# A Mamba block and a routed mixture of experts on one core: two of eight drive products moved to TensorE, and the start and end of the scan stage reordered

## The reference, cut to what matters

```python
h = layernorm(layernorm(x)) * g + b
x_in, z = split(h @ W_in)                      # 512 channels each
u = silu(causal_depthwise_conv(x_in, taps=4) + conv_b)
dt, B, C = split(u @ W_xproj)                  # 64, 16 and 16 columns
delta = softplus(dt @ W_dt + b_dt)
s[n] = exp(delta * A[n]) * s[n] + delta * u * B[n]     # 16 states n, over time
y = sum_n s[n] * C[n] + u * D
x1 = x + layernorm(x) + (y * silu(z)) @ W_out
# experts: each row of layernorm(x1) goes to its best 2 of 8 experts,
# relu(row @ W1 + b1) @ W2 + b2, weighed by a softmax of the two logits
out = x1 + layernorm(mixed + row) * gamma + beta
```

## Time and profile before

| | us |
|---|---|
| median of three runs (2540.58 to 2542.79) | 2542.03 |
| the profiled execution, its own time | 2553.05 |
| its span, first to last instruction | 2551.3 |
| first scan starts | 74.19 |
| last gate of the scan stage starts | 1890.67 |
| first tile of the experts is read | 1954.25 |
| busy: PE, DVE, ACT, POOL | 2055.1, 2123.9, 1408.2, 1965.7 |
| mean granted TensorE clock | 0.90 |

### The profile page before, as it was taken

How to read it: one execution, slowest core, us unless ns; L and a number is a source line. 1 busy time by engine, 2 the same in 40 slices (tenths; PEclk the granted TensorE clock), 3 DMA queues, 4 the chain that set the end, 5 groups by cost and what they waited for, 6 DMA issues and landing times. The chain is left out here.

```text
span 2551.3 us, 41205 instructions
## 1 busy us (share of the span) xinstructions
PE 2055.1 (81%) x11191; PEld 1561.7 (61%) x11192; DVE 2123.9 (83%) x3249; ACT 1408.2 (55%) x2909; POOL 1965.7 (77%) x1233
## 2 busy tenths in 40 slices
PE   6769687796968787796968787796754999999988
PEld 2446465564646555565646555564653999999973
DVE  1899999999999999999999999999962556555657
ACT  4666766767676766766675776766431222222216
POOL 1899899999999999999999999999962222222227
PEclk9889898898989798898989898898765999999999
DMA  3240413224040413214041413314034777777769
GB/s 102 87 150 10 141 57 126 85 91 157 18 167 33 151 51 124 102 74 166 21 155 35 149 60 116 113 55 166 11 120 139 223 227 230 227 227 231 227 197 332
DMA packets 177827, 328.42 MB, mean 129 GB/s; under 512 B 19539, under 2 KB 100979, under 8 KB 177556
## 3 DMA queue, kind: packets, MB, share of 16 engines
q1 hardware_dynamic: 147172, 274.00, 33.6%
q0 software_dynamic: 12624, 34.62, 3.6%
q10 hardware_dynamic: 17888, 18.11, 2.1%
HBM read 272.25 MB, written 54.41 MB: 128 GB/s over the span
## 5 line engine op out<-in xcount | busy, mean ns | idle before, releaser
L729 POOL TENSOR_TENSOR dbu<-du,bb 128x1024 f32<-128x1024 f32 x512 | 1199.0, 2355 | 13.4 <-DVE ps_a L564 9.0
L960 ACT ACTIVATE ps_a<-dl,a_neg 128x512 f32<-128x512 f32 x1024 | 683.0, 683 | 151.4 <-DVE wd L577 75.5
L1162 PEld LDWEIGHTS ps_y<-ident,wd 128*128 128x128 f32 x2816 | 376.5, 158 | 112.9 <-issue 82.9
L1162 PE MATMUL ps_y<-ident,wd 128*128 128x128 f32 x2816 | 425.6, 299 | 16.5 <-DVE wd L577 16.5
L564 DVE TENSOR_TENSOR_SCAN ps_a<-ps_a,carry,dbu 128x512 f32<-128x512 f32 x352 | 437.5, 1276 | 0.1
L1440 POOL DMA_INDIRECT eo_scratch<-ow,idx x135 | 129.9, 962 | 391.3 <-DVE ow L1394 385.4
L577 DVE TENSOR_TENSOR wd<-ps_a,rows_c 128x1024 f32<-128x1024 f32 (+1 forms) x384 | 426.9, 1112 | 0.0
L564 DVE TENSOR_TENSOR_SCAN ps_a<-ps_a,dbu 128x512 f32<-128x512 f32 x352 | 417.1, 1216 | 4.1 <-ACT ps_a L960 3.7
L746 POOL TENSOR_TENSOR wp<-ss,rows_c 128x1024 f32<-128x1024 f32 (+1 forms) x192 | 382.0, 1990 | 15.2 <-DVE ss L564 7.5
L1549 PE MATMUL e_ps_h<-xT,w 128*128 128x128 f32 x2160 | 264.9, 276 | 0.0
L1380 DVE TENSOR_SCALAR e_hT<-e_ps_h,b_turned 128x128 f32<-128x128 f32 x540 | 152.1, 344 | 134.7 <-PE e_ps_h L1549 133.7
(11 more groups left out here) (166 smaller groups left out, 2798.5 us busy)
## 6 DMA issues: line engine op xcount, KB each, us to landing
w<-in_L_ffn_W_dram SPq DMA_DIRECT2D x135, 512.0 KB
bb<-b_scratch SPq DMA_DIRECT2D x128, 512.0 KB, 4.3
rows_c<-b_scratch SPq DMA_DIRECT2D x128, 512.0 KB, 6.6
xt<-xs_scratch SPq DMA_DIRECT2D x135, 129.0 KB
ee<-eo_scratch SPq DMA_DIRECT2D x64, 256.0 KB, 7.2
xb<-in_L_attn_x_dram SPq DMA_DIRECT2D x16, 512.0 KB, 3.7
hx<-in_L_attn_x_dram SPq DMA_DIRECT2D x16, 512.0 KB, 5.4
x_scratch<-hx SPq DMA_DIRECT2D x16, 512.0 KB, 3.3
```

The lines of the kernel that those rows point to most:

```text
L729: pool.tensor_tensor(dbu[:, k % NBU], du[:, g % 2, :].unsqueeze(1).broadcast_to([P, 2, CH]), bb[:, 2 * m:2 * m + 2, :], ALU.mult).then_inc ...
L960: act.activation(ps_a[:, bank(k), :], dl[:, g, :], ACT.Exp, scale=a_neg[:, g, n:n + 1]).then_inc(exp_done, 1)
L1162: ins = pe.matmul(ps_y[:, i, :], wd[:, s % NWD, h, i * P:(i + 1) * P], ident[:], start=False, stop=False, is_transpose=True, skip_group_ch ...
```

## The change

- **Drive of four states from turned rows.** For the states 4, 5, 10 and 11 (the pairs 2 and 5, `BMS`) GpSimd makes no product. TensorE turns delta * u once a tile ("turnu", four transposes), ScalarE copies it to `duT`. Once a chunk TensorE turns the B rows ("bturn"), and ScalarE scales the identity by them, giving 16 diagonals (`diagonals`). `drive` multiplies the turned rows by the diagonals, 16 matrix products a tile, into the PSUM bank that took the decay before; the decay of these states goes to the ring `dbu` in SBUF. The scan takes them with their places exchanged.
- **State 15 is held.** VectorE has five pairs a tile to weigh, GpSimd three pairs, where it had two pairs and a single. Which bank a pair has now changes from tile to tile.
- **Residual and its statistics.** The residual row is added by TensorE with the identity inside "out"; ScalarE takes it out with its sum, and its squares with a second pass (`stats_x1` moves from VectorE to ScalarE).
- **Order.** `STEADY` and all offsets are new. The routing follows one chunk behind, not two. In the first tiles of chunk 0 the list `START` holds what no longer stands ahead of the first scan (z, the next h and x).
- **Start.** The first convolution is done on VectorE (`first_conv`); weights are loaded in three groups with semaphores of their own, some from ScalarE's queue, and W_in in two halves; ahead of the first scan stand two softplus and half the diagonals.
- **End.** `out_part` sums three of the four groups of the last output projection ahead of its last gate; the last "back" has a PSUM bank of its own; the second choice's rows of the last chunk have a buffer (`stage_b`); the padding transfers are issued half by SyncE, half by ScalarE.

The diff, cut to its core:

```diff
+    BMS = (2, 5)
+    NTP = len(BMS)
     HB = N // 2
+    NB = HB - NTP
...
-    DIRECT = (1, 4, 7, 10, 13, 15)
+    DIRECT = (1, 4, 7, 10, 13)
+    ND = len(DIRECT)
...
+        bb = sb("bb", [P, 2 * NB, CH])
+        dg = sb("dg", [P, NTP, 2, NT, P])
+        duT = sb("duT", [P, NT, P])
+        bT = sb("bT", [P, NT, NTP, 2])
...
+        stage_b = zt[:, NC % 2].rearrange("p i d -> p (i d)")[:, 0:NT * XW].rearrange("p (i d) -> p i d", i=NT)
...
-        FIRST = [("h", 0), ("h", 1), ("x", 0), ("x", 1), ("x", 2), ("x", 3), ("conv", 0), ("conv", 1), ("conv", 2),
-                 ("conv", 3), ("dbc", 0), ("dt", 0), ("dt", 1), ("z", 0), ("dt", 2), ("z", 1), ("dt", 3), ("z", 2),
-                 ("z", 3)]
...
+        FIRST = [("h", 0), ("h", 1), ("x", 0), ("x", 1), ("x", 2), ("x", 3), ("dbc", 0), ("bturn", 0), ("dt", 0),
+                 ("dt", 1), ("turnu", 0)]
+        START = [("z", 0, 0, 0, 1, 1), ("z", 1, 0, 0, 1, 2), ("z", 2, 0, 1, 1, 3), ("z", 3, 0, 2, 1, 4),
+                 ("h", 0, 1, 4, 1, 2), ("h", 1, 1, 5, 1, 2), ("x", 0, 1, 8, 1, 2), ("x", 1, 1, 10, 1, 2),
+                 ("turnu", 1, 0, 13, 1, 2)]
+        START_DIAGONALS = (2, 3)
+        END = [("back", 2, 0, 54, 1, 2)]
+        XL_LAST = NC * SG - 14
+        OUT_EARLY = NC * SG - 5
+        STEADY = [("h", 0, 1, 0, 1, 3), ("h", 1, 1, 1, 1, 5), ("x", 0, 1, 4, 2, 3), ("back", 3, -1, 6, 1, 2),
+                  ("dt", 2, 0, 9, 1, 2), ("out", 0, -1, 10, 1, 4), ("turnu", 1, 0, 10, 1, 5),
+                  ("out", 1, -1, 14, 2, 4), ("x", 1, 1, 17, 1, 5), ("conv", 0, 1, 18, 2, 2), ("conv", 1, 1, 21, 2, 5),
+                  ("x", 2, 1, 24, 2, 3), ("x", 3, 1, 25, 1, 4), ("dt", 3, 0, 29, 1, 2), ("conv", 2, 1, 27, 3, 5),
+                  ("turnu", 2, 0, 33, 1, 4), ("conv", 3, 1, 30, 4, 8), ("turnx", 0, -1, 37, 1, 4),
+                  ("turnx", 1, -1, 37, 1, 4), ("logit", 0, -1, 40, 1, 0), ("dbc", 0, 1, 41, 1, 4),
+                  ("back", 0, 0, 42, 1, 3), ("bturn", 0, 1, 43, 1, 3), ("rank", 0, -1, 43, 1, 1),
+                  ("back", 1, 0, 45, 1, 3), ("turnu", 3, 0, 47, 1, 1), ("dt", 0, 1, 48, 1, 1), ("dt", 1, 1, 49, 1, 2),
+                  ("z", 0, 1, 53, 2, 2), ("z", 1, 1, 54, 2, 4), ("z", 2, 1, 56, 2, 5), ("turnu", 0, 1, 59, 1, 2),
+                  ("z", 3, 1, 59, 2, 4), ("back", 2, 0, 60, 1, 4)]
+        HALO_AT = 0
...
+        DIAGONALS = (53, 59, 64, 64)
+        DRIVE = (4, 5, 10, 10)
+        KEEP_EARLY = (2, 9)
...
+            def first_conv(g):
+
+                dve.wait_ge(*emptied("x", g, 0))
+                dst = xslot(0, g)
+                dve.tensor_scalar(dst, xin[:, g, 0:CH], cw[:, g, 0:1], cb[:, g:g + 1], ALU.mult, ALU.add
+                                  ).then_inc(conv_step, 1)
+                for k in range(1, TAPS):
+                    dve.wait_ge(conv_step, TAPS * g + k)
+                    dve.scalar_tensor_tensor(dst, xin[:, g, k:k + CH], cw[:, g, k:k + 1], dst, ALU.mult, ALU.add
+                                             ).then_inc(conv_step, 1)
...
+                if n // 2 in BMS:
+                    dve.wait_ge(tb_done, driven(t, n))
+                elif n % 2 == 0:
+                    dve.wait_ge(dbu_done, products(t, n // 2))
...
-                dve.tensor_tensor_scan(dst, ps_a[:, bank(k), :], dbu[:, k // 2 % NBU, n % 2, :], init,
-                                       ALU.mult, ALU.add).then_inc(scan_done, 1)
+                pair = ps_a[:, bank(k), :], dbu[:, k // 2 % NBU, n % 2, :]
+                decay, drive = reversed(pair) if n // 2 in BMS else pair
+                dve.tensor_tensor_scan(dst, decay, drive, init, ALU.mult, ALU.add).then_inc(scan_done, 1)
...
-                if t <= LAST:
+                if t <= LAST and m not in BMS:
                     times_b(t, m)
...
+            def stats_x1(q, step):
+
+                if step == 0:
+                    for j in range(2):
+                        act.wait_ge(*emptied("out", j, q))
+                    if q > 0:
+                        act.wait_ge(prm1, q)
+                    act.mul(nm[:, 1, :], sums[:], -1.0 / D).then_inc(lnr_step, 1)
+                else:
+                    act.wait_ge(lnr_step, 2 * q + 1)
+                    if q > 0:
+                        if q < NC - 1:
+                            act.wait_ge(scat, 16 * 2 * NT * q)
+                        act.wait_ge(proj_full, full("turnx", 1, q - 1))
+                        act.wait_ge(proj_full, full("out", 1, q - 1))
+                    junk = rows_from(q, 1)
+                    for i in range(NT):
+                        ins = act.activation(junk[:, i, 0:D], hx[:, i, :], ACT.Square, bias=nm[:, 1, i:i + 1],
+                                             accum_out=sqs[:, i:i + 1])
+                    ins.then_inc(lnr_step, 1)
+
...
+                elif kind == "turnu":
+                    act.wait_ge(tb_done, 2 * NTP * (q * G + g))
+                    act.copy(duT[:].rearrange("p i d -> p (i d)"), src).then_inc(taken, 1)
+                elif kind == "bturn":
+                    act.wait_ge(dg_done, NTP * q)
+                    rows = src[:, 0:NT * 2 * N].rearrange("p (i n) -> p i n", i=NT)
+                    for p, b in enumerate(BMS):
+                        ins = act.copy(bT[:, :, p, :], rows[:, :, 2 * b:2 * b + 2])
+                    ins.then_inc(taken, 1)
+                elif kind == "out":
+                    for i in range(2 * g, 2 * g + 2):
+                        ins = act.activation(hx[:, i, :], src[:, (i - 2 * g) * D:(i - 2 * g + 1) * D], ACT.Copy,
+                                             accum_out=sums[:, i:i + 1])
+                    ins.then_inc(taken, 1)
                 else:
                     act.copy(zt[:, q % 2, :, g * P:(g + 1) * P], src.rearrange("p (i d) -> p i d", i=NT)
                              ).then_inc(taken, 1)
+
+            def diagonals(q, j):
...
+            def diagonals(q, j):
+
+                p = j // 2
+                act.wait_ge(*emptied("bturn", 0, q))
+                if q > 0:
+                    act.wait_ge(tb_done, 2 * (NTP * (G * q - 1) + p) + 2)
+                for i in range(2 * (j % 2), 2 * (j % 2) + 2):
+                    for h in range(2):
+                        ins = act.activation(dg[:, p, h, i, :], ident[:], ACT.Copy, scale=bT[:, i, p, h:h + 1])
+                if j % 2 == 1:
+                    ins.then_inc(dg_done, 1)
...
+                if n // 2 in BMS:
+                    dst = dbu[:, k // 2 % NBU, n % 2, :]
+                    if k // 2 >= NBU:
+                        act.wait_ge(scan_done, k - n % 2 - 2 * NBU + 2)
...
+                    if q == NC - 1:
+                        if part == parts - 1:
+                            ins = out_part(q, g, range(G - 1, G))
+                    for ik in range(2 * G * part // parts, 2 * G * (part + 1) // parts) if q < NC - 1 else ():
                         i, k = divmod(ik, G)
                         ins = pe.matmul(dst[:, i * D:(i + 1) * D], zt[:, q % 2, 2 * g + i, k * P:(k + 1) * P],
-                                        wout[:, k, :], start=(k == 0), stop=(k == G - 1))
+                                        wout[:, k, :], start=(k == 0), stop=False)
+                        if k == G - 1:
+                            pe.wait_ge(xl_done, q + 1)
+                            ins = pe.matmul(dst[:, i * D:(i + 1) * D], ident[:], hx[:, 2 * g + i, :], start=False,
+                                            stop=True)
                 if part == parts - 1:
                     ins.then_inc(proj_full, 1)
...
+            def out_part(q, j, groups):
+
+                for i in range(2):
+                    dst = proj("out", j, q)[:, i * D:(i + 1) * D]
+                    for k in groups:
+                        ins = pe.matmul(dst, zt[:, q % 2, 2 * j + i, k * P:(k + 1) * P], wout[:, k, :],
+                                        start=(i == 0 and k == 0), stop=(k == G - 1), skip_group_check=True)
+                    if groups[-1] < G - 1:
+                        pe.matmul(dst, ident[:], hx[:, 2 * j + i, :], start=False, stop=False, skip_group_check=True)
+                return ins
 
...
+            def drive(t, p, h):
+
+                c, g = t // G, t % G
+                k = t * N + 2 * BMS[p] + h
+                if h == 0:
+                    pe.wait_ge(*emptied("turnu", g, c))
+                    pe.wait_ge(dg_done, NTP * c + p + 1)
+                    for j in (before(k), before(k + 1)):
+                        if j is not None:
+                            pe.wait_ge(*released(j))
+                            if j // SG % 2 == 0:
+                                pe.wait_ge(carry_act, kept(j))
+                for i in range(NT):
+                    ins = pe.matmul(ps_a[:, bank(k), i * P:(i + 1) * P], duT[:, i, :], dg[:, p, h, i, :], start=True,
+                                    stop=True)
+                ins.then_inc(tb_done, 1)
 
...
+                if at == OUT_EARLY:
```

(5 more changed lines are left out.)

401 lines of the change are left out of this document (221 added, 180 removed), and 3 rows, old and new, of the table STEADY.

## The result

The changed kernel takes 2513.9 us in the median of four runs (2512.39 to 2514.97), the kernel before 2542.4 in four of the same comparison: ratio 0.9875, 95% interval 0.986 to 0.989. It is faster by 1.25%, where 2381 us was forecast and 2342 to 2450 given as range. The profiled execution took 2514.33, its span is 2512.3, 39.0 less than before; as the profiled execution of before lay 11 us above its median, about 10 of these 39 are no gain; in which part of it the extra time lies isn't known.

A forecast was written before the change was run, and what follows sets the result against it. VectorE and GpSimd, both nearly full in the scan stage, were taken as the bound. Gains of 112 (sixteen chunks), 28 (start) and 21 us (tail) sum to 161: 2542 - 161 = 2381 us, range 2342 to 2450.

The forecast's parts named there:

- Start: Before the first scan: fewer weights ahead, convolution on VectorE and a new order bring it to 45 us; 28 us less.
- Tail: From last scan to first expert tile: routing and output sums done earlier, separate buffer for second choice; 21 us less.
- VectorE's floor: Steady chunk: VectorE loses weighings, residual additions and statistics, 5.0 us, and needs 104.9 us of the chunk.
- 100 at full clock: Steady chunk: TensorE's load rises from about 82 by 18.3 us for drives, transposes and residual, staying under VectorE's 104.9.
- The steady chunk: Scan stage: a chunk falls from 114.3 to 107.3 us, between 104.9 and 109.3; 112 us over sixteen chunks.
- The 1 us a chunk for GpSimd's pile in the fourth tile: Scatters pile up there: GpSimd needs 31 us against VectorE's mean 26; the product ring covers some 9; 1 us charged.
- 2.0 us of slack for the drive of scan 4: After scan 15, TensorE's chain to scan 4's drive takes 5.5 us while VectorE has 7.5 us of other work.
- Sixteen chunks gain the same: Scan stage: the shorter edge chunks gain as much as steady ones, 16 x (114.3 - 107.3) = 112 us.
- The scan stage does not move: Rival: VectorE's relief becomes idle behind ScalarE or the drives, chunk stays 114.3, only ends gain; 2493 us; chance 0.05.
- TensorE takes over: Rival: half-clock stretches stay, so TensorE sets the chunk at about 111.5 us; 2448 us in all; chance 0.20.
- Slower by the drive: Rival: scan 4 waits for its drive over 3.1 us a tile; chunk 127, about 2640 us; chance 0.04.
- Transposes at low clock: Rival: 300 transposes a chunk run at low clock, TensorE needs 133 us a chunk; 2797 us; chance 0.01.

The follow-up runs named there:

- the second x piece: Changed kernel with the second x projection issued right behind the first instead of behind the out projections; alone 2510.4 us, ratio 0.9864 to the kernel before.
- S and X: Changed kernel with the second choice's four scatters moved to the next chunk's second tile and the second x projection right behind the first; 2466.6 us, ratio 0.9692.

## Why the prediction was wrong

- *Start*, forecast 28: 28.2, first scan at 45.94 (45). Right.
- *Tail*, forecast 21: 24.5. The first tile is read 44.5 us after the last scan (48). Right, mis-sized by 3.5.
- *VectorE's floor* 104.9: 105.3. *GpSimd* 97.3: 98.1. *ScalarE* 91: 87.1, although a diagonal is 0.39, not 0.35. Neighbours overlap (32 diagonals of 392 ns occupy 10.0 us, not 12.5), which the sum took off for VectorE and not here. A driven scan keeps its duration (1220 and 1278 ns), as put down. *TensorE* 100 at full clock: 104.0 busy at a clock of 0.98 in the run with the scatters moved, so 102 at full clock. Clock 0.96 in the chunk (over 0.95). The terms hold.
- *The steady chunk*, forecast 107.3: 114.3. Here is the step that failed: loads were summed over the chunk and compared there, and the second tile's surplus was left "to be worked off in the third". The third can't take it, being full on both engines (29.1 and 29.3), and the first is fuller still (TensorE 30.4, where 30 was given to the second, which has 27.1). What does pass a gate, GpSimd's pile, lands in the first window. By window, the fullest engine of each gives 30.4 + 27.1 + 29.3 + 25.8 = 112.5 from the same loads; the 1.8 us left, and a part of the 30.4, are waits and low clock. That doubled drives cost window by window, and that halved z gave nothing, shows on the chip that the place of the load counts and not its total.

  The kernel before had it already. These are the windows of one of its chunks; the fullest engine (GpSimd, VectorE, VectorE, GpSimd) is busy 28.3 + 27.05 + 30.7 + 28.2 = 114.2 of 114.4, where the largest total over the chunk is 111.8. The prediction read two tiles, each full on another engine, and then added up the chunk.

```profile
868.30:896.60 28.30, 26.95 (x130) 17.39 (x130) 26.65 (x29) 14.23 (x24) 28.30 (x15) 0.93 0.07 21
896.60:923.65 27.05, 25.60 (x140) 18.27 (x140) 27.05 (x32) 20.16 (x34) 26.70 (x13) 1.00 0.00 1
923.65:954.53 30.88, 23.64 (x113) 16.14 (x112) 30.68 (x43) 18.47 (x41) 28.10 (x19) 0.89 0.32 105
954.53:982.69 28.16, 15.07 (x92) 13.19 (x90) 26.81 (x26) 23.02 (x38) 28.16 (x15) 0.76 0.73 255
```
- *The 1 us a chunk for GpSimd's pile in the fourth tile*, and 2.0 us of slack for the drive of scan 4: the pile was seen (31 us were named), its price was wrong. The weighing comes late, TensorE stands 3.2 us (up to 4.2 in other chunks), then runs at 0.50 for 3.4, and has no pause up to the next gate. Moving four scatters gave 1.75 us a chunk; the second x piece could give 1.4 only after that.
- *Sixteen chunks gain the same*: the first chunk grew by 9.9, for what left the start (z, the next h and x) has to be done in it; the two after it by 1.5 and 3.4.
- *The rivals.* "The scan stage does not move" (0.05) described the outcome best: chunk 114.3, though its 2493 is 21 below the time: 15 for the edge chunks and 10 for the slow profiled execution of before, less some 5 for the better end and the experts. Its reason was another one. "TensorE takes over" (0.20) had the right engine and a wrong price, by total load at half clock: 111.5. Slower by the drive: all driven scans together wait 7.0 us for TensorE in eight tiles, 0.9 a tile, far from 3.1. The 2640 given for it counts the ends twice; a chunk of 127 would make 2542 + 16 x 12.7 - 49 = 2696. The forecast doesn't rest on it. Transposes at low clock: eight take 1.09 at a clock of 1.00, so no; the rule of the Trainium skill (TensorE: Matmul & The Clock Gate, Part 4: PE-mode transpose) that had given this rival is not borne out here either.

What stays open is the rest of the way. S and X need 111.1 us a chunk with VectorE busy 105.2. Its waits in two of these chunks, the longest ones:

```profile
DVE zt L634 <- PE ps_y L1316: 3.4, 2, 2.0
DVE ps_a L612 <- PE ps_a L1343: 3.1, 3, 1.4
DVE ss L612 <- issue: 1.9, 2, 1.0
```

Two of the three are TensorE's, full in the second window (27.05 of 27.05 us); less drive work shortened that window, fewer taps didn't, so what is to leave it isn't clear from its load. Only the fourth has room, and for the pieces that were moved there TensorE or VectorE had to wait for ScalarE. That a better order exists isn't excluded; none was found.

## What to carry to other kernels

Where engines hand small buffers to each other in a written order, compare their loads between two hand-overs, not over a period: the period is at least the sum of the fullest engine's time in each, and the traces here came to 112.5 of 114.3 and 114.2 of 114.4. Do it first on the trace of the kernel before. That an engine is always busy in a stretch doesn't mean that taking any of its work shortens it. A wait of TensorE just ahead of its fullest stretch costs twice, by its length and by the low clock around it. Before moving a long piece on an in-order engine, look at what it overlaps there and how many results the consumer has in hand; three such moves cost 5 to 11 us a chunk here, and two others gave 3.1 together.

## What the runs showed of the hardware

TensorE's granted clock was 0.55 in a wait of 3.17 us and 0.50 in the 3.43 us of full work after it, then 0.99 (0.50 and 1.00 are 1.2 and 2.4 GHz). It fell 0.3 us into that wait; in the 6.2 us before, TensorE had been busy 3.8. In the slow stretch eight transposes took 1.97 us and eight drive records 1.92; without that wait the clock was 1.00 there and they took 1.09 and 1.06. A ScalarE instruction with a sum has a second record, 195 ns for the read of the accumulator, beside 373 for the copy of 256 columns; on VectorE the same read took 82. A matmul drive in PSUM with the decay in SBUF costs a scan no more than the reverse (1220 and 1278 ns against 1211 and 1271).
